# Up- and down-sampling of 1024 images on TensorE: the down-sampling goes from 128x64 to 64x64 array tiles

## The chip, the cores and the metric

One core of a Trainium2 chip runs the kernel. Its time is device time in microseconds, the median of several runs. The core has TensorE (matmuls, results in the PSUM banks), VectorE, ScalarE and GpSimd (POOL) for element work, and SyncE (SP), which here only issues DMAs. VectorE and ScalarE read PSUM; GpSimd doesn't.

## What is computed

Input x is (2, 512, 256, 256), float32. Two layers follow each other. The first adds a plane of sines to every channel:

```python
lin = jnp.einsum('oc,chw->ohw', W, coord) + b[:, None, None]   # coord: x and y in -1..1
fourier = jnp.sin(lin)
return x + fourier[None]
```

The second adds a bias per channel, up-samples by 2 with a 12-tap filter along both axes, applies a leaky ReLU (slope 0.2, times sqrt(2)), and down-samples by 2 with another 12-tap filter along both axes:

```python
out = input + bias[None, :, None, None]
out = _sep_upfirdn(out, upf, UP, 1, UP_PAD)          # 256x256 -> 512x512
out = jax.nn.leaky_relu(out, NEG_SLOPE) * FLRELU_SCALE
out = _sep_upfirdn(out, down_filter, 1, DOWN, DOWN_PAD)   # 512x512 -> 256x256
```

## The kernel before, in words

**The unit of work is an image**, one of the two batch entries of a channel; m = 2c + n is its number, c the channel and n the batch entry, 1024 in all. Each filter pass is a matmul with a band matrix: the data is the stationary operand (so that a pass also transposes), the band of filter taps (`up_band`, `down_band`, made once by VectorE, lines 369 to 381) is the moving one, and only the columns that a block of rows can reach are streamed.

**The stages of an image.** GpSimd adds x_raw and the plane f_sb into x_sum (line 245). `up_rows` (line 463) up-samples it into the two banks a_ps; ScalarE copies them to a_sb (`copy_a`). `up_cols` (line 472) up-samples a_sb into the four banks y_ps, two (a pair) at a time. ScalarE makes leak = slope x y and VectorE takes z = max(gain x y, leak) (line 392). `down_rows` (line 483) down-samples z into the bank p_ps, twice per image (i = 0, 1), and VectorE copies each half to p_rows (`copy_p`, line 400). `down_cols` (line 491) down-samples p_rows into the bank o_ps, ScalarE copies it to o_out (`copy_o`), and SP stores it.

**Array tiles.** `up` (line 439) puts 64 rows by 128 columns on the array: two tiles, one for each half of the rows. It runs in two steps (step 0 and 1), so that the two row halves never write the same bank at once; step 1 waits for a semaphore that step 0 has raised (`a_half`, `y_half`). `down` (line 428) puts 128 rows by 64 columns: two tiles, one for each half of the columns, which write different partitions of the same bank; it needs no steps. `DN_SPAN` gives the output columns that 128 input rows reach (68 or 72), `UP_SPAN` those of 128 rows going up; `up` halves the latter to 132 to 138 columns for 64 rows. All of this is float32, and the profile shows each such matmul as two loads and two matmuls.

**The plane f** is a product: sin(a+b) = sin a cos b + cos a sin b, with the bias added. `tables` (line 339) computes the sines and cosines on VectorE and ScalarE for 128 channels at a time, splits each in a high and a low float32r part (lines 360, 361), and SP saves ten rows per channel to `trig_dram` (`save_rows`). Per channel SP loads the ten rows (`load_f_rows`), `sines` (line 454) makes f in two float32r matmuls into the bank o_ps, which it shares with `down_cols`, and ScalarE copies it to f_sb (`copy_f`).

**The order.** There is no scheduler: every engine has a list written out by hand (`slot` in each engine's block), and semaphores with counted values tie them together. TensorE's slot of image m is: `up_cols` pair 0 step 0; `up_rows` of image m+1 step 0; `up_cols` pair 0 step 1; `up_cols` pair 1 step 0; `up_rows` m+1 step 1; `up_cols` pair 1 step 1; for n = 0 `sines` of channel c+1; `down_rows` of image m-1, i = 0; `down_cols` of image m-2; `down_rows` of m-1, i = 1. VectorE's slot: `leaky` 0, 1 of m, `copy_p` 0 of m-1, `leaky` 2, 3 of m, `copy_p` 1 of m-1. ScalarE's: `copy_o` of m-3, `leaky` 0, 1, `copy_a` of m+1, `copy_f` of c+1, `leaky` 2, 3. TensorE's loop (line 533) has a body of two channels, four images, and runs 254 times. `up_cols` waits for z_done, so that VectorE has read the y_ps banks of the image before. The instructions of a matmul on different tiles can pass each other on TensorE; on the other engines all goes in the order of the list.

## Time and profile before

| | us |
|---|---|
| median of 3 runs | 6572.86 (6572.68 to 6572.97) |
| the profiled execution | 6572.63 |
| its span, first to last instruction | 6570.9 |
| TensorE matmuls busy | 6509.3 (99%) |
| VectorE busy | 4002.7 (61%) |
| ScalarE busy | 3980.8 (61%) |
| GpSimd busy | 1303.7 (20%) |
| HBM traffic | 558 MB, 85 GB/s |

A row of the groups names the line, the engine, the operation, the tile written and those read, the shapes and the count; then busy us and the mean ns of one, and the idle time of the engine just before, with what ended it. PE is TensorE's matmul, PEld its weight load. Matmuls are pipelined and their ends are modelled: their starts are measured, so lengths of blocks are read here from start to start. TensorE's granted clock was full (2.4 GHz) in all slices.

### The profile page before, as it was taken

The numbers are of one execution on the slowest core, as the hardware profiler recorded it, in microseconds if no ns is written. First come the engines' busy times: TensorE is split into PE (matmuls) and PEld (weight loads), VectorE is DVE, ScalarE is ACT, GpSimd is POOL, SyncE is SP. The second block draws the span as 40 slices with busy tenths as digits, with TensorE's granted clock in tenths as the row PEclk, the third lists the DMA queues.
The fourth block names the chain that finished last, engine by engine and source line by source line (L and its number), as shares of the span: only waits on it lengthen the run. The fifth ranks groups of instructions, "written<-read, shape, count | busy, mean of one in ns | idle before, by whom it ended". The sixth has DMA issues, their size and how long they took to land.

```text
span 6570.9 us, 361569 instructions
## 1 busy us (share of the span) xinstructions
PE 6509.3 (99%) x148480; PEld 6210.1 (95%) x148480; DVE 4002.7 (61%) x6218; ACT 3980.8 (61%) x7688; POOL 1303.7 (20%) x1041
## 2 busy tenths in 40 slices
PE   6999999999999999999999999999999999999999
PEld 6999999999999999999999999999999999999999
DVE  6666666666666666666666666666666666666665
ACT  4666666666666666666666666666666666666665
POOL 2111111111111111111111111111111111111111
PEclk9999999999999999999999999999999999999999
DMA  3222222222222222222222222222222222222222
GB/s 121 85 84 84 85 85 85 84 84 83 83 84 85 85 85 85 85 85 83 85 85 85 85 83 83 83 84 85 85 85 85 85 85 83 84 85 85 85 84 78
DMA packets 580065, 558.27 MB, mean 85 GB/s; under 512 B 40400, under 2 KB 574928, under 8 KB 580048
## 3 DMA queue, kind: packets, MB, share of 16 engines
q1 hardware_dynamic: 580048, 558.02, 27.2%
q8 instruction: 14, 0.23, 0.0%
q14 instruction: 3, 0.02, 0.0%
HBM read 278.94 MB, written 278.92 MB: 85 GB/s over the span
## 4 chain that ended last, share of the span: by engine, by line
PE 99%; DVE 1%; DMA 0%; SPq 0%; issue 0%; ACT 0%; DVEq 0%; POOL 0%; POOLq 0%
PE p_ps L433 34%; PE y_ps L449 32%; PE o_ps L433 15%; PE a_ps L449 14%; PE o_ps L459 3%; DVE up_band L377 0%; DVE angle L354 0%; DVE angle L352 0%; DVE phase L344 0%; ACT trig L258 0%; DVE trig_parts L361 0%; DVE angle L356 0%; DVE turns L348 0%; DVE turns L350 0%; DVE trig_parts L360 0%
## 5 line engine op out<-in xcount | busy, mean ns | idle before, releaser
L392 DVE SCALAR_TENSOR_TENSOR z<-y_ps,leak 128x512 f32<-128x512 f32 x4096 | 2629.3, 684 | 1749.8 <-ACT leak L278 1749.8
L278 ACT ACTIVATE leak<-y_ps 128x512 f32<-128x512 f32 x4096 | 2280.0, 623 | 2108.0 <-PE y_ps L449 2107.6
L449 PE MATMUL y_ps<-up_band,a_sb 64*128 64x138 f32 (+2 forms) x32768 | 2539.2, 282 | 1.4 <-ACT a_sb L271 1.3
L433 PE MATMUL p_ps<-down_band,z 128*64 128x68 f32 (+1 forms) x65536 | 2440.8, 227 | 1.7 <-DVE p_rows L400 1.7
L245 POOL TENSOR_TENSOR x_sum<-x_raw,f_sb 128x512 f32<-128x512 f32 x1024 | 1291.3, 1283 | 5235.6 <-ACT f_sb L264 5226.3
L433 PEld LDWEIGHTS p_ps<-down_band,z 128*64 128x64 f32 x65536 | 2156.2, 137 | 160.6 <-DVE z L392 1.0
L449 PEld LDWEIGHTS y_ps<-up_band,a_sb 64*128 64x128 f32 x32768 | 2163.4, 186 | 75.1 <-issue 1.5
L400 DVE COPY p_rows<-p_ps 128x512 f32<-128x512 f32 x2048 | 1416.2, 691 | 802.3 <-PE p_ps L433 699.1
L449 PE MATMUL a_ps<-up_band,x_sum 64*128 64x138 f32 (+2 forms) x16384 | 1306.6, 275 | 28.6 <-POOL x_sum L245 28.5
L433 PE MATMUL o_ps<-down_band,p_rows 128*64 128x68 f32 (+1 forms) x32768 | 1170.2, 224 | 0.8 <-DVE p_rows L400 0.8
L449 PEld LDWEIGHTS a_ps<-up_band,x_sum 64*128 64x128 f32 x16384 | 1132.9, 187 | 29.4 <-POOL x_sum L245 29.0
L271 ACT COPY a_sb<-a_ps 128x512 f32<-128x512 f32 x2048 | 1109.4, 606 | 5.2 <-PE a_ps L449 5.2
L433 PEld LDWEIGHTS o_ps<-down_band,p_rows 128*64 128x64 f32 x32768 | 1082.4, 137 | 0.9 <-DVE p_rows L400 0.9
L283 ACT COPY o_out<-o_ps 128x512 f32<-128x512 f32 x1024 | 600.6, 587 | 432.5 <-PE o_ps L433 432.5
L264 ACT COPY f_sb<-o_ps 128x512 f32<-128x512 f32 x512 | 323.4, 632 | 0.3 <-PE o_ps L459 0.3
L459 PE MATMUL o_ps<-f_rows 10*128 10x256 f32 x1024 | 254.0, 326 | 25.8 <-DVE up_band L381 25.4
L459 PEld LDWEIGHTS o_ps<-f_rows 10*128 10x128 f32 x1024 | 149.9, 183 | 91.3 <-DVE up_band L381 25.4
L258 ACT ACTIVATE trig<-angle 128x1024 f32<-128x1024 f32 x4 | 4.2, 1056 | 40.5 <-DVE angle L356 40.5
L233 POOL TENSOR_SCALAR bias_wide<-ones,bias_high 128x256 fp32r<-128x256 f32 x4 | 5.7, 1436 | 3.7 <-DVE bias_low L334 3.7
L361 DVE TENSOR_TENSOR trig_parts<-trig,trig_parts 128x1024 f32 (+1 forms) x4 | 5.8, 1448 | 0.5
L360 DVE CAST trig_parts<-trig 128x1024 f32 (+1 forms) x4 | 2.8, 703 | 4.8 <-ACT trig L258 4.8
L377 DVE SCALAR_TENSOR_TENSOR up_band<-up_ones,up_taps,up_band 128x268 f32<-128x268 f32 x11 | 5.5, 498 | 0.4
(28 smaller groups left out, 43.0 us busy)
## 6 DMA issues: line engine op xcount, KB each, us to landing
x_raw<-in_x_dram SPq DMA_DIRECT2D x1024, 256.0 KB, 3.1
out_dram<-o_out SPq DMA_DIRECT2D x1024, 256.0 KB, 2.5
f_rows<-trig_dram SPq DMA_DIRECT2D x512, 20.0 KB
trig_dram<-trig_parts SPq DMA_DIRECT2D x32, 256.0 KB, 2.5
trig_dram<-ones SPq DMA_DIRECT2D x4, 256.0 KB, 2.4
trig_dram<-bias_wide SPq DMA_DIRECT2D x4, 256.0 KB, 2.5
up_taps<-in_L_conv_up_filter_dram SPq DMA_DIRECT2D x1, 6.0 KB, 2.3
down_taps<-_L_conv_down_filter_dram SPq DMA_DIRECT2D x1, 6.0 KB, 2.4
```

Of the source, the lines that this page charges most:

```text
L233: nc.gpsimd.tensor_scalar(bias_wide[:, t, 0, :], ones[:, 0, :], bias_high[:, t:t + 1].bitcast(f32), None, ALU.mult)
L245: nc.gpsimd.tensor_tensor(x_sum[n][:, :, :], x_raw[n][:, :, :], f_sb[:, :, :], ALU.add).then_inc(x_summed, 1)
L264: nc.scalar.copy(f_sb[:, :, :], o_ps[:, :, :]).then_inc(f_copied, 1)
L271: last = nc.scalar.copy(a_sb[n][:, t, :], a_ps[t][:, :])
L278: nc.scalar.mul(leak[i % 2][:, :], y_ps[i][:, :], SLOPE * GAIN).then_inc(leak_done, 1)
L283: nc.scalar.copy(o_out[n][:, :, :], o_ps[:, :, :]).then_inc(o_copied, 1)
L361: nc.vector.tensor_tensor(parts[:, 1, :, :], trig[:, :, :], parts[:, 0, :, :].bitcast(f32), ALU.subtract).then_inc(rows_ready, 1)
L392: nc.vector.scalar_tensor_tensor(z[n][:, i, :], y_ps[i][:, :], GAIN, leak[i % 2][:, :], ALU.mult, ALU.max).then_inc(z_done, 1)
L400: nc.vector.tensor_copy(p_rows[n][:, 2 * i:2 * i + 2, :], p_ps[:, :, :]).then_inc(p_copied, 1)
L433: last = nc.tensor.matmul(out_ps[half * HALF:(half + 1) * HALF, lo:hi], data[:, t, col:col + HALF], down_band[:, band:band + hi - lo], sta ...
L449: last = nc.tensor.matmul(outs[o][:, lo:hi], data[row, k, (at + o) * P:(at + o + 1) * P], up_band[row, band:band + hi - lo], start=step == ...
L459: last = nc.tensor.matmul(o_ps[:, t, :], f_rows[:, t * P:(t + 1) * P], f_rows[:, H:H + WID], start=True, stop=True)
```

## The change

Constants, banks and rows:

- Down-sampling is cut to 64 input rows: `DN_SPAN` has, for each of the four 128-row tiles, two spans of 36 or 40 output columns. `step_of` replaces `up` and `down`: it puts 64 rows by `cols` columns on the array, 128 columns for up-sampling, 64 (`DOWN_COLS`) for down-sampling, and runs in two steps as `up` did. Every step begins with `pe.sem_inc(steps_begun, 1)`. Up-sampling's spans are the same as before.
- p_ps gets two banks, p_ps[0] and p_ps[1], both filled only when both steps of `down_rows` have run; ScalarE copies the first (`copy_p0`), VectorE the second (`copy_p1`). The bank o_ps is gone: `down_cols` writes the left half of the two banks a_ps, and waits that ScalarE and VectorE have copied a out of them.
- a is copied by ScalarE (`copy_a0`) and VectorE (`copy_a1`), one bank each.
- The split in high and low parts is gone: f has three plain float32 rows (sine, cosine and one for the bias) instead of ten. They are loaded twice, to partitions 0 and 64 of f_rows, the rest of which GpSimd sets to zero once. `sines` runs on four 64x64 tiles into the left halves of y_ps[0] and y_ps[1], waits for z_done of the running image's first two banks, and VectorE copies it (`copy_f`). SP saves 4 times per group of channels, not 10, and loads the f rows behind the x loads and stores of a channel.

```diff
-    DN_SPAN = [(0, 68, 4), (60, 132, 0), (124, 196, 0), (188, 256, 0)]
+    DN_SPAN = [[(max(0, 32 * g - 4), min(H, 32 * g + 36), max(0, 32 * g - 4) + 4 - 64 * (g // 2)) for g in (2 * k, 2 * k + 1)]
+               for k in range(UT)]
...
-        p_ps = pb("p_ps", [P, 2, H])
-        o_ps = pb("o_ps", [P, HT, WID])
+        p_ps = [pb(f"p_ps{o}", [P, 2, H]) for o in range(2)]
```

TensorE, the common step, sines and the down-sampling:

```diff
+            def step_of(cols, outs, data, band, spans, at, where, ks, step, fresh=True):
+
+                pe.sem_inc(steps_begun, 1)
+                for k in ks:
                     for rows in range(2):
                         o = rows ^ step
                         row = slice(rows * HALF, (rows + 1) * HALF)
...
+                        lo, hi, start = spans[k][rows]
+                        for part in range(0, P, cols):
+                            col = (at + o) * P + part
+                            last = nc.tensor.matmul(outs[o][part:part + cols, lo:hi], data[row, where[k], col:col + cols],
+                                                    band[row, start:start + hi - lo],
+                                                    start=fresh and step == 0 and k == 0,
+                                                    stop=step == 1 and k == len(spans) - 1, skip_group_check=True)
                 return last
 
...
+            def sines(c, z_from):
+
+                pe.wait_ge(f_rows_loaded, 32 * c + 32)
+                reached(pe, z_done, z_from)
+                pe.sem_inc(steps_begun, 1)
                 for t in range(HT):
...
+                    row = slice(t * HALF, (t + 1) * HALF)
+                    for part in range(0, P, DOWN_COLS):
+                        col = t * P + part
+                        last = nc.tensor.matmul(y_ps[t][part:part + DOWN_COLS, 0:WID],
+                                                f_rows[row, col:col + DOWN_COLS], f_rows[row, H:H + WID],
+                                                start=True, stop=True, skip_group_check=True)
                 last.then_inc(f_made, 1)
...
+            def up_cols(m, n, pair, step, f_done=None, a_from=None):
+
                 outs = y_ps[2 * pair:2 * pair + 2]
                 if step == 0:
...
+                    if f_done is not None:
+                        pe.wait_ge(f_copied, f_done)
+                    else:
+                        reached(pe, z_done, 4 * m - 2 + 2 * pair)
...
+            def down_cols(m, n, step, a_done=None):
+                outs = [a_ps[t][:, 0:WID] for t in range(HT)]
+                if step == 0:
+
+                    if a_done is not None:
+                        pe.wait_ge(a0_copied, a_done)
+                        pe.wait_ge(a1_copied, a_done)
```

TensorE's new slot:

```diff
                 m = 2 * c + n
                 if y:
...
+                    up_cols(m, n, 0, 0, c + 2 if n == 0 and f_before else None, m + 1 if first else None)
                     up_cols(m, n, 1, 0)
                 if a_next:
+                    up_rows(m + 1, 1 - n, 0, first)
+                if y:
+                    up_cols(m, n, 0, 1)
+                if a_next:
                     up_rows(m + 1, 1 - n, 1)
                 if y:
                     up_cols(m, n, 1, 1)
-                if f_next and n == 0:
-                    sines(c + 1)
                 if p:
-                    down_rows(m - 1, 1 - n, 0)
+                    down_rows(m - 1, 1 - n, 0, 0)
+                    down_rows(m - 1, 1 - n, 0, 1)
                 if o:
-                    down_cols(m - 2, n, c + 2 if f_done is None else f_done)
+                    down_cols(m - 2, n, 0, m + 2 if a_next else None)
                 if p:
-                    down_rows(m - 1, 1 - n, 1)
+                    down_rows(m - 1, 1 - n, 1, 0)
+                if o:
+                    down_cols(m - 2, n, 1)
+                if f_next and n == 1:
+                    sines(c + 2, 4 * m + 2)
+                if p:
+                    down_rows(m - 1, 1 - n, 1, 1)
```

VectorE's new slot, with the copy of f:

```diff
+            def copy_f(c):
+
+                dve.wait_ge(f_made, c + 1)
+                reached(dve, x_summed, 2 * c)
+                for t in range(HT):
+                    last = nc.vector.tensor_copy(f_sb[:, t, :], y_ps[t][:, 0:WID])
+                last.then_inc(f_copied, 1)
+
+            def slot(c, n, a_next=True, f_next=True, y=True, p=True):
                 m = 2 * c + n
+                if a_next:
+                    copy_a1(m + 1, 1 - n)
                 if y:
                     leaky(m, n, 0)
                     leaky(m, n, 1)
-                if p:
-                    copy_p(m - 1, 1 - n, 0)
+                if f_next and n == 1:
+                    copy_f(c + 2)
                 if y:
                     leaky(m, n, 2)
                     leaky(m, n, 3)
                 if p:
-                    copy_p(m - 1, 1 - n, 1)
-
+                    copy_p1(m - 1, 1 - n)
+
```

ScalarE's new slot is `leaky` 0, `copy_a0` of m+1, `leaky` 1, 2, 3, `copy_o` of m-2 (two instructions of 256 columns), `copy_p0` of m-1. TensorE's loop body stays two channels.

## Rows read from the trace of the kernel before

**Rows 1.** The page: busy shares, the chain, and p_ps's group.

```profile
PE 6509.3 (99%) x148480; PEld 6210.1 (95%) x148480; DVE 4002.7 (61%) x6218; ACT 3980.8 (61%) x7688; POOL 1303.7 (20%) x1041
...
PE 99%; DVE 1%; DMA 0%; SPq 0%; issue 0%; ACT 0%; DVEq 0%; POOL 0%; POOLq 0%
...
L433 PE MATMUL p_ps<-down_band,z 128*64 128x68 f32 (+1 forms) x65536 | 2440.8, 227 | 1.7 <-DVE p_rows L400 1.7
```

**Rows 2.** TensorE's waits: engine, line, waited for: us, times, longest.

```profile
PE a_ps L449 <- POOL x_sum L245: 28.5, 2, 26.6
PE o_ps L459 <- DVE up_band L381: 25.4, 1, 25.4
PE p_ps L433 <- DVE p_rows L400: 1.7, 2, 0.9
```

**Rows 3.** Windows of two images: us, busy us (count) by engine, clock.

```profile
3000.03:3006.13 6.10, 6.10 (x148) 5.90 (x145) 3.88 (x7) 3.63 (x7) 0.40 (x1) 1.00 0.44 129
3006.13:3012.74 6.61, 6.61 (x151) 6.23 (x147) 3.87 (x7) 4.12 (x8) 2.13 (x2) 1.00 0.12 43
```

**Rows 4.** Timeline of one image: start us, us, instruction, count.

```profile
3000.04 0.73 PE L449 MATMUL y_ps<-up_band,a_sb 64*128 64x132 f32 x8
...
3001.06 1.10 PE L449 MATMUL y_ps<-up_band,a_sb 64*128 64x132 f32 x16
...
3001.98 0.64 PE L449 MATMUL a_ps<-up_band,x_sum 64*128 64x132 f32 x8
...
3002.55 1.29 DVE L392 SCALAR_TENSOR_TENSOR z<-y_ps,leak 128x512 f32<-128x512 f32 x2 [1.70 <-ACT leak L278]
...
3003.02 1.19 PE L433 MATMUL p_ps<-down_band,z 128*64 128x68 f32 x32
...
3004.04 1.14 PE L433 MATMUL o_ps<-down_band,p_rows 128*64 128x68 f32 x32
3004.26 0.69 DVE L400 COPY p_rows<-p_ps 128x512 f32<-128x512 f32 x1 [0.42 <-PE p_ps L433]
...
3005.02 1.18 PE L433 MATMUL p_ps<-down_band,z 128*64 128x68 f32 x32
...
3006.13 0.54 PEld L449 LDWEIGHTS y_ps<-up_band,a_sb 64*128 64x128 f32 x8
```

**Rows 5.** Timeline windows that end behind the first 2, 4, 6 loads.

```profile
3003.01 0.14 PEld L433 LDWEIGHTS p_ps<-down_band,z 128*64 128x64 f32 x2
3003.01 0.20 PEld L433 LDWEIGHTS p_ps<-down_band,z 128*64 128x64 f32 x4
3003.01 0.26 PEld L433 LDWEIGHTS p_ps<-down_band,z 128*64 128x64 f32 x6
...
3003.02 0.28 PE L433 MATMUL p_ps<-down_band,z 128*64 128x68 f32 x2
...
3006.13 0.19 PEld L449 LDWEIGHTS y_ps<-up_band,a_sb 64*128 64x128 f32 x2
3006.13 0.30 PEld L449 LDWEIGHTS y_ps<-up_band,a_sb 64*128 64x128 f32 x4
```

**Rows 6.** Timeline of the setup: the split of the sines on VectorE.

```profile
32.59 0.69 DVE L360 CAST trig_parts<-trig 128x1024 f32 x1 [1.24 <-ACT trig L258]
33.43 1.22 DVE L361 TENSOR_TENSOR trig_parts<-trig,trig_parts 128x1024 f32 x1
```

**Rows 7.** The page's groups of VectorE and ScalarE: busy us, mean ns.

```profile
L392 DVE SCALAR_TENSOR_TENSOR z<-y_ps,leak 128x512 f32<-128x512 f32 x4096 | 2629.3, 684 | 1749.8 <-ACT leak L278 1749.8
L278 ACT ACTIVATE leak<-y_ps 128x512 f32<-128x512 f32 x4096 | 2280.0, 623 | 2108.0 <-PE y_ps L449 2107.6
L400 DVE COPY p_rows<-p_ps 128x512 f32<-128x512 f32 x2048 | 1416.2, 691 | 802.3 <-PE p_ps L433 699.1
L271 ACT COPY a_sb<-a_ps 128x512 f32<-128x512 f32 x2048 | 1109.4, 606 | 5.2 <-PE a_ps L449 5.2
```

**Rows 8.** Queues, and DMA issues with the median us to landing.

```profile
q8 instruction: 14, 0.23, 0.0%
...
x_raw<-in_x_dram SPq DMA_DIRECT2D x1024, 256.0 KB, 3.1
out_dram<-o_out SPq DMA_DIRECT2D x1024, 256.0 KB, 2.5
```

## What the change is expected to do, written before it ran

> **What bounds the kernel now.** I read the busy shares and the chain first: TensorE is busy 99% of the span and carries 99% of the chain that ended last, nearly all of it on lines 449 (up-sampling) and 433 (down-sampling) [rows 1]. The waits confirm it: what TensorE waited for sums to under 60 us, and 54 of them fall once, before the first sums [rows 2]. So in steady state only two things can move the time: how long TensorE's own stretches last, and a wait that is new to it. Next the windows: an image (one batch entry of one channel) takes 6.10 us, one with the sine matmuls 6.61 [rows 3], a channel 12.71, 512 channels 6507 of the 6570.9 us span. VectorE and ScalarE are busy only 3.9 and 3.6 to 4.1 us of each image [rows 3], which looks like slack but says nothing of when they are done.
>
> The timeline of one image gives the order: the up-sampling blocks (48 records, 0.46 for every 8) go from 3000.04 to about 3002.9; three down-sampling blocks of 32 records start at 3003.02, 3004.04 and 3005.02; the next image starts at 3006.13 [rows 4]. An f32 matmul is two records (two loads, two matmuls): 65536 records of p_ps are 1024 images with 32 matmuls [rows 1]. The down part is thus 3.11 us: 48 rounds of about 0.061 (two records at once, one on each half of the columns; the round of the first stretch is (3004.04 - 3003.02 - 0.055)/16 = 0.060) and 0.15 for draining the array and the first load.
>
> **The price that decides: a weight load.** What a 64x64 round costs is not in the trace, but its two ingredients are. Columns: 138 columns on 64x128 tiles go through in a round of 0.115 (16 records in 0.92, two at once [rows 4]), 0.83 ns a column, so a 40-column record streams in 0.033. Loads: at the head of the down block two 64-column loads end 0.14 after their start, four 0.20, six 0.26 [rows 5]: each half of the array takes its next load 0.055 to 0.06 after the last one. The first of these steps cannot come from streaming, since nothing streamed yet. For 128 columns the same step is 0.11 (two end at 0.19, four at 0.30) [rows 5], so a load costs by its columns, 0.86 ns each. Before, 70 columns (0.058) just cover the 64-column load. In the changed kernel 40 columns (0.033) don't, and the load has become the longer of the two.
>
> **The change, part by part.**
> 1. Down-sampling. An image's 48 matmuls of 68 or 72 columns become 96 of 36 or 40, 192 records. Four at a time that is 48 rounds, as many as before: only the round's length changes. If loads of four tiles run side by side (the trace shows it for two column halves and for two row halves, not for four), a round is 0.055 to 0.060; I take 0.057. 48 x 0.057 = 2.74 + 0.15 = 2.89 against 3.11: 0.22 saved per image, 0.44 per channel. The bounds from rows are 0.033 (streaming alone) and 0.110 (only two loads at a time).
> 2. Sines. Two records of 256 columns and a mode of their own cost 6.61 - 6.10 = 0.51 per channel [rows 3]. Now four f32 matmuls of 256 columns on four tiles, two passes of 256 x 0.83 = 0.21, 0.43 together, in the mode of their neighbours: 0.08 saved.
> 3. Up-sampling keeps its spans, tiles and number: 0. Its order changes (both first halves go ahead); each second half still has a block between itself and what it waits for, 0.46 or more, against some 0.2 from last column to a reader's start (p_ps block ends at 3004.04, VectorE's copy starts 4.26 [rows 4]): hidden. The new p and o half steps have a 0.46 block between them too. If that cover were gone, each would cost up to 0.2.
> 4. Copies. VectorE loses one p copy and gets half of a (one 0.69 each), and f in two of 256 columns; per channel 12 x 0.605 + 0.68 = 7.9 of 12.7 (0.605 is the step from one 512-column instruction to the next: two end 1.29 after the first starts, one takes 0.69 [rows 4, 7]). ScalarE has 4 leaks, one a, one p and two o halves: 4 x 0.62 + 2 x 0.61 + 2 x 0.35 = 4.4 of 6.1 at most [rows 7]. POOL does the same sums. Throughput of each is covered. o now waits for a_sb to be out of a_ps: a_ps is full 2.4 us into the image, both copies are done at 3.3 (0.2 and 0.69 later), and the o step starts at 2.9 + 0.2 + 2 x 0.456 = 4.0: hidden, with 0.7 to spare.
> 5. Semaphore steps: 12 or 13 more sequencer instructions per image, and 290 records per image become about 480. Now a block's 32 loads and 32 matmuls are fed in 0.97 [rows 4]; then it must be in 0.456. In 0.02 us two loads and two matmuls start [rows 5], so the engine accepts them in bursts; I take 0, bound 0.1 per image (+100 us in all), and a gain is excluded.
> 6. Setup: the split of the sines in two parts goes, 0.7 + 1.2 to 1.3 us for each of four groups on VectorE [rows 6], which stand before the first sum: -8 us. SP: 4 saves for 10, f rows in two DMAs for one, now issued behind the next x loads and stores; the rows are needed 12 us later and a landing takes some 3 [rows 8]: 0.
>
> Sum without waits: 12.71 - 0.44 - 0.08 = 12.19 per channel, -266 us.
>
> **7. The wait that the change adds.** f now goes through y_ps[0..1], is made by `sines` late in the second image of each channel (behind the o half steps, ahead of the last p block), and is copied by VectorE. In VectorE's order `copy_f` stands between `leaky` 1 and `leaky` 2 of that same image. VectorE is through with `leaky` 1 some 4.5 us into the image and then waits for f until about 6.0, with the `leaky` 2, 3 and the p copy of this image queued behind it, although their y is ready. TensorE needs them at once: `up_cols` step 0 of pair 0 in the next image waits for f_copied, that of pair 1 for all four z. Set the end of the sines to 0:
> - copy_f starts at 0.22 (the 0.22 of point 3), two copies of 256 columns 2 x 0.34 (half of the 0.605 step and some for its start), f_copied at about 1.0;
> - z2 starts at 0.90, z3 at 1.50, ends at 2.19 (0.69 [rows 7]), seen by TensorE at 2.24;
> - TensorE without waits: last p block to 0.46, drain and first load 0.20 (from 3006.13 back to the end of the columns, and 0.11 for the 128-column load), so up_cols pair 0 at 0.55 and pair 1 at 1.12.
> So pair 0 waits 0.48 and pair 1 the rest, 1.12 together, and 0.1 for a weight load laid bare behind the second wait: 1.2 per channel, +625 us. Nothing is late behind that: the rest of the image runs as the sum has it, since its z and copies have slack again.
>
> 12.19 + 1.22 = 13.41, +0.70 per channel, x 512 = +358; 6572.6 (the profiled execution's own time, beside a median of 6572.9) + 358 - 8 = 6923, and with a little of point 5, **6930 us**. A round of 0.055 gives 6830, one of 0.060 and the full point 5 give 7170.
>
> **Rivals.**
> - **Instruction memory (B), 7250.** The queue of instructions moved 14 packets, 0.23 MB, in the whole run [rows 8]: the loop's body is fetched once and kept. That body is 4 images x 290 = 1160 instructions; the new one is 4 x 480 + 32 = 1952 and some 100 for semaphores and registers. If it isn't kept, each of 254 passes waits for its first part: a DMA's way from issue to landing is 2.5 to 3.1 us [rows 8], during which the 1.1 of point 7 passes too. Net 1.0 to 1.6 a pass, +250 to +400 on 6930: 7180 to 7330. The trace shows a body of 1160 kept and no more. [...]
> - **Loads don't bind (C), 6380 to 6490: the other side.** If a 64x64 tile's load is cheaper than a half array's, a round is 0.036 to 0.045. The down part is then 1.7 to 2.2 and the sum without waits 10.2 to 11.0, but z of the upper half then arrives late in every image: the chain from the last y block over ScalarE's leaks and VectorE's z to the next image's pair 1 costs 0.5 in each image beside point 7. With the same durations, step by step as in point 7, a channel takes 12.33 to 12.54. It decides from a round under 0.046. Against it: loads cost by their columns in rows 5, and the tile's columns stay 64. The Trainium skill, "TensorEngine Tiling (Array Packing)", Tiling Modes, says that different tiles can load and multiply in parallel, its Theoretical Speedup gives up to 2x for each dimension that is 64 or less, and its PSUM Bottleneck names the copies as what may bind next. By that rule alone this case would hold.
> - **The wait of point 7 is hidden (E), 6520 to 6580.** If VectorE got z2 and z3 done ahead of f, pair 1 wouldn't wait: 12.65 per channel. The order in the code speaks against it.
> - **Four tiles don't run at once (D), about 9300.** If only two of the loads or records go side by side, a round is 0.110: 48 x 0.05 more per image. The trace shows two at once along either side of the array, and a program order of four instructions per tile that is overtaken for one other tile; three others would have to be reached.
>
> **How the numbers follow.** The forecast (A) 0.43, B 0.23, C 0.13, E 0.06, D 0.15. A's own range is 6830 to 7170. The range that leaves out D and some of C and of the ends is 6400 to 7400. About 0.2% is what a measurement of this kernel can tell from no change; E straddles that. Faster 0.17 (C and most of E), same 0.02, slower 0.81.
>
> **What would show it.** In the timeline of the changed kernel: blocks of 32 records at 0.44 to 0.48 apart in the down part (right: A; 0.3: C; 0.9: D); VectorE idle before copy_f for some 1.5 us each channel, released by the sines; waits of y_ps on VectorE's f_sb (about 0.5 x 512) and z (about 0.6 x 512) in TensorE's list; windows near 6.1 and 7.3 for the two images of a channel. The instruction queue's packets stay near 20 (A) or go to thousands (B), with a gap at the start of every fourth image. I am wrong if the loads of a tile don't cost by columns, or if the last two z are not behind f.

## The result and the profile after

The changed kernel takes **11206.6 us** (11195.7 to 11216.6, 4 runs) against 6572.9 before (6572.7 to 6574.1): the ratio is **1.705, 95% interval 1.702 to 1.708**. The forecast was 6930 with a range of 6400 to 7400; the sign was right, the size wrong by more than 4000 us. Of the 4634 us lost, 4066 come from something that the forecast's sum put at nothing, as the first experiment shows; the other 568 are the loss that it describes.

The page of the changed kernel (busy shares, clock, the instruction queue, the chain):

```profile
PE 8078.5 (72%) x249856; PEld 7506.8 (67%) x249856; DVE 4281.8 (38%) x7232; ACT 4104.5 (37%) x8200; POOL 1308.7 (12%) x1038
...
PEclk9888888888888888888888888888888888888888
...
q8 instruction: 2300, 37.68, 1.3%
...
PE 69%; issue 27%; DVE 4%; DVEq 1%; ACT 0%; DMA 0%; SPq 0%; POOL 0%; ACTq 0%; POOLq 0%
```

TensorE, 99% busy before [rows 1], is busy 72%. The chain now has 27% "issue": time in which TensorE waited for nothing that the profile shows. And the instruction queue, which moved 14 packets before [rows 8], moves 2300. TensorE's waits (engine, line, waited for: us in total, times, longest), which summed to under 60 us before [rows 2]:

```profile
PE y_ps L451 <- issue: 870.4, 253, 3.9
PE y_ps L466 <- issue: 765.3, 509, 2.1
PE a_ps L451 <- issue: 637.4, 512, 1.8
PE p_ps L451 <- issue: 629.4, 491, 1.9
PE y_ps L451 <- DVE f_sb L402: 114.0, 258, 1.1
PE y_ps L451 <- DVE z L388: 61.8, 132, 1.7
```

The four "issue" rows sum to 2902.5 us, 11.4 for each of the 254 passes of the loop; what the forecast was about, the waits for f and z, is 176 us. A stretch of TensorE's timeline shows where the gaps are (start us, us, instruction, count; in brackets the idle time ahead). It begins with the branch at the loop's end:

```profile
6025.40 1.02 PE L451 MATMUL p_ps<-down_band,z 64*64 64x40 f32 x24
6029.62 2.19 PE L451 MATMUL y_ps<-up_band,a_sb 64*128 64x132 f32 x16 [3.19 <-issue]
6031.55 1.16 PE L451 MATMUL a_ps<-up_band,x_sum 64*128 64x132 f32 x8
6032.45 1.17 PE L451 MATMUL y_ps<-up_band,a_sb 64*128 64x132 f32 x8
...
6037.33 0.63 PE L451 MATMUL a_ps<-down_band,p_rows 64*64 64x36 f32 x26
6039.21 0.32 PE L451 MATMUL a_ps<-down_band,p_rows 64*64 64x40 f32 x6 [1.24 <-issue]
...
6045.05 0.60 PE L451 MATMUL p_ps<-down_band,z 64*64 64x36 f32 x27 [1.36 <-issue]
```

Three things are to be seen. First, the gap at 6029.62 stands at the branch; those at 6039.21 and 6045.05 break off in the middle of a block of equal matmuls (32 of a_ps are cut in 26 and 6), where no wait stands in the code. My reading is that TensorE has run out of instructions; the experiments test it. Second, apart from the branch, the down-sampling part with the sines in it is where this happens. Third, the up-sampling blocks behind the long gap follow each other at 0.90 us and not at the 0.46 of before [rows 4]: the granted clock, 1.00 in all of before, is 0.867 here, and a pass from branch to branch has 0.81:

```profile
6025.73:6070.76 45.03, 33.17 (x994) 30.78 (x988) 16.59 (x28) 16.03 (x32) 5.08 (x4) 0.81 0.17 50
...
6025.73:6035.36 9.63, 6.43 (x70) 6.08 (x64) 3.23 (x7) 1.89 (x4) 1.95 (x2) 0.50 0.10 32
```

(us; busy us and count of PE, PEld, DVE, ACT, POOL; clock; DMA share and GB/s.) The low clock, 0.50, comes in two stretches of this pass: up to 6035.36, where it is already down at the branch, behind a stop in the sines (1.65 us, up to 6024.89), and again from 6048.95 to 6055.83 (0.52, TensorE busy for 6.64 us), behind a stop of 1.83 in the sines. The shorter stops at 6039.21 and 6045.05 leave it at 1.00. In the two stretches TensorE is busy for 13.1 us; at an up block's 0.46 for 0.90 about half of that, some 6.4 us, is the price of the clock (an estimate from these rows). This pass of two channels took 45.0 us; before, it was 25.4. Its instruction packets start at 6026.74, 6030.28, 6036.68, 6042.62, 6046.30, 6050.14, 6057.85, 6063.48 and 6067.18: nine, of 16.4 KB each (37.68 MB by 2300), for a body of some 2,040 instructions, taking 0.93 to 1.28 us each. TensorE goes on 2.2 to 2.9 us after the start of a packet it was waiting for (6057.85 to 6060.05: 2.20; 6036.68 to 6039.21: 2.53; 6026.74 to 6029.62: 2.88).

### The profile page after: what moved, and what is told of

The parts are those of the page before. It is cut to its first block, busy times and chain, and to the rows that moved or that the text cites. A ratio compares the mean times of both kernels' runs of the same rounds, so it can differ in the third digit from the quotient of the medians.

```text
span 11214.8 us, 576531 instructions
## 1 busy us (share of the span) xinstructions
PE 8078.5 (72%) x249856; PEld 7506.8 (67%) x249856; DVE 4281.8 (38%) x7232; ACT 4104.5 (37%) x8200; POOL 1308.7 (12%) x1038
## 3 DMA queue, kind: packets, MB, share of 16 engines
q8 instruction: 2300, 37.68, 1.3%
## 4 chain that ended last, share of the span: by engine, by line
PE 69%; issue 27%; DVE 4%; DVEq 1%; ACT 0%; DMA 0%; SPq 0%; POOL 0%; ACTq 0%; POOLq 0%
PE y_ps L451 25%; PE a_ps L451 22%; PE p_ps L451 18%; PE y_ps L466 4%; DVE f_sb L402 2%; DVE z L388 1%; DVEq L137 0%; DVEq L385 0%; DVEq L425 0%; DVE up_band L367 0%; DVE angle L346 0%; DVE angle L348 0%; DVE phase L338 0%; ACT trig L258 0%; DVE turns L342 0%
## 5 line engine op out<-in xcount | busy, mean ns | idle before, releaser
L451 PE MATMUL y_ps<-up_band,a_sb 64*128 64x138 f32 (+2 forms) x32768 | 3377.5, 341 | 1046.3 <-issue 870.4
L451 PEld LDWEIGHTS y_ps<-up_band,a_sb 64*128 64x128 f32 x32768 | 2944.7, 240 | 1165.0 <-issue 1142.3
L451 PE MATMUL p_ps<-down_band,z 64*64 64x40 f32 (+1 forms) x131072 | 2811.3, 228 | 631.1 <-issue 629.4
L451 PEld LDWEIGHTS p_ps<-down_band,z 64*64 64x64 f32 x131072 | 2490.8, 137 | 885.5 <-issue 733.5
L451 PE MATMUL a_ps<-down_band,p_rows 64*64 64x40 f32 (+1 forms) x65536 | 1553.2, 226 | 638.4 <-issue 637.4
L381 DVE COPY a_sb<-a_ps 128x512 f32<-128x512 f32 x1024 | 707.7, 691 | 3358.2 <-PE a_ps L451 3358.2
L451 PEld LDWEIGHTS a_ps<-down_band,p_rows 64*64 64x64 f32 x65536 | 1313.5, 135 | 698.9 <-issue 698.9
L277 ACT COPY o_out<-a_ps 128x256 f32<-128x256 f32 x2048 | 662.0, 375 | 1915.0 <-PE a_ps L451 1915.0
L466 PE MATMUL y_ps<-f_rows 64*64 64x256 f32 x4096 | 540.4, 449 | 789.4 <-issue 765.3
L284 ACT COPY p_rows<-p_ps 128x512 f32<-128x512 f32 x1024 | 609.9, 596 | 1220.6 <-PE p_ps L451 1220.4
L395 DVE COPY p_rows<-p_ps 128x512 f32<-128x512 f32 x1024 | 701.2, 685 | 918.9 <-PE p_ps L451 918.9
```

Source lines behind the costliest of these rows:

```text
L277: last = nc.scalar.copy(o_out[n][:, t, :], a_ps[t][:, 0:WID])
L284: nc.scalar.copy(p_rows[n][:, 0:2, :], p_ps[0][:, :, :]).then_inc(p0_copied, 1)
L381: nc.vector.tensor_copy(a_sb[n][:, 1, :], a_ps[1][:, :]).then_inc(a1_copied, 1)
L395: nc.vector.tensor_copy(p_rows[n][:, 2:4, :], p_ps[1][:, :, :]).then_inc(p1_copied, 1)
L451: last = nc.tensor.matmul(outs[o][part:part + cols, lo:hi], data[row, where[k], col:col + cols], band[row, start:start + hi - lo], start=f ...
L466: last = nc.tensor.matmul(y_ps[t][part:part + DOWN_COLS, 0:WID], f_rows[row, col:col + DOWN_COLS], f_rows[row, H:H + WID], start=True, sto ...
```

## The experiments

A body's size is given in TensorE's instructions, counted in the traces from branch to branch with the semaphore and register instructions. The kernel before has 1,208 (1,210 below), the changed kernel 2,036 (2,040). The expectations were written with somewhat higher figures: 1,030 for 1,019, 2,050 for 2,036, 2,430 for 2,414 and 1,880 for 1,811.

**One channel in the loop's body.** The changed kernel with a body of some 1,020.

```diff
-    PE_CHANNELS = 2
+    PE_CHANNELS = 1
```

> The changed kernel with TensorE's loop body cut from two channels to one (PE_CHANNELS = 1; every instruction and wait is the same, the body is some 1,030 instructions in place of some 2,050). Theory 1 (instruction memory: the body of two channels is fetched again in each pass, 2300 packets, and TensorE runs dry because a block of 64x64 instructions is used up faster than the next one comes): the queue of instructions falls from 2300 packets to some 20, the gaps put down to issue go, the clock is back at 1.0, and the time is that of the sum without rival B, 6930 (6830 to 7170). Theory 2 (64x64 tiles themselves are slow, or the added waits are, and the fetches are beside the point): stays above 9000. Inside theory 1: the rounds of four loads are 0.055 to 0.060 us, and TensorE waits some 1.1 us per channel for VectorE's f_sb and z.

Measured: 7140.9 us (7139.5 to 7143.4), 1.087 times before (1.085 to 1.088), clock 0.998. The instruction queue, TensorE's waits and the part of the timeline around the second sum of a channel:

```profile
q8 instruction: 19, 0.31, 0.0%
...
PE y_ps L451 <- DVE f_sb L402: 314.1, 511, 1.1
PE y_ps L451 <- DVE z L388: 235.9, 511, 1.4
```

```profile
3001.74 0.73 PE L451 MATMUL y_ps<-up_band,a_sb 64*128 64x132 f32 x8 [0.61 <-DVE f_sb L402]
3002.93 0.73 PE L451 MATMUL y_ps<-up_band,a_sb 64*128 64x132 f32 x8 [0.46 <-DVE z L388]
3003.47 0.66 PE L451 MATMUL a_ps<-up_band,x_sum 64*128 64x132 f32 x8
...
3005.45 1.14 PE L451 MATMUL p_ps<-down_band,z 64*64 64x36 f32 x64
...
3007.80 0.65 PE L451 MATMUL p_ps<-down_band,z 64*64 64x36 f32 x32
3008.38 1.20 PE L451 MATMUL y_ps<-up_band,a_sb 64*128 64x132 f32 x16
...
3013.25 0.65 PE L451 MATMUL a_ps<-down_band,p_rows 64*64 64x36 f32 x32
3013.78 0.66 PE L466 MATMUL y_ps<-f_rows 64*64 64x256 f32 x8
3014.23 0.65 PE L451 MATMUL p_ps<-down_band,z 64*64 64x36 f32 x32
3015.49 0.73 PE L451 MATMUL y_ps<-up_band,a_sb 64*128 64x132 f32 x8 [0.61 <-DVE f_sb L402]
```

With the shorter body nothing is fetched again, the gaps are gone and so is the low clock: one number in the code is worth 4066 us. What is left, +568, is the case that the forecast describes (13.76 per channel on the average, 3001.74 to 3015.49 here; its own range was 6830 to 7170). The 4066 split by the two pages: gaps 2903, TensorE's busy time 8078.5 - 6516.9 = 1562 more for the same instructions (the lower clock: 6.1 a pass, where the estimate above is 6.4), and 374 less waiting for f and z (176 for 550): 4091 in sum, 25 off.

**The copy of f last.** On top of that, VectorE's copy of f behind `leaky` 3.

```diff
-                if f_next and n == 1:
-                    copy_f(c + 2)
                 if y:
                     leaky(m, n, 2)
                     leaky(m, n, 3)
+                if f_next and n == 1:
+                    copy_f(c + 2)
```

> As e1, and VectorE copies f behind leaky 2 and 3 of its image, not ahead of them (one line of its slot moved). Point 7 of the prediction: the second of the two waits (for z, some 0.64 and a load of 0.1 per channel) goes, the first (for f_sb, 0.48) stays: 12.65 to 12.7 us per channel, 380 us under e1, about 6550. Rival: the waits cost nothing or lie elsewhere: same time as e1.

Measured: 6766.0 us (6763.5 to 6767.7), 1.030 (1.028 to 1.031); 13.03 per channel. The step, 375 us, is the 380 expected; the level is 215 above the number, because the run it started from was. The wait for z is gone (2.3 us in all), that for f stays at 313.8: TensorE asks for f first.

**Pair 1 first.** On top of that, `up_cols` step 0 of pair 1 ahead of that of pair 0 in the first image of a channel (and y_half waits to suit), so that f has one more block of time.

```diff
-                    pe.wait_ge(y_half, 2 * m + pair + 1)
+                    pe.wait_ge(y_half, 2 * m + (2 if n == 0 else pair + 1))
...
+                    if n == 0 and not first:
+                        up_cols(m, n, 1, 0)
+                        up_cols(m, n, 0, 0, c + 2 if f_before else None)
...
```

> As e2, and in the first image of a channel TensorE begins with pair 1 of up_cols and does pair 0, which waits for f, second (the waits for y_half are raised to match). If the rest of point 7 holds, the wait for f_sb (0.48 per channel) is covered by the 0.46 block of pair 1: 12.2 us per channel, about 6310, which would be 4% under the kernel before. Rival: something else of the down part (sequencer instructions, a longer round) holds it: 6450 to 6600.

Measured: 6543.4 us (6541.5 to 6545.0), 0.9955 (0.9938 to 0.9971): under before, but by 29 us, not 260; in the size a miss. The waits on f and z are gone (1.7 and 2.3 us in all) and another has come, at the branch:

```profile
PE y_ps L451 <- issue: 87.0, 506, 0.2
```

```profile
3004.73 0.65 PE L451 MATMUL p_ps<-down_band,z 64*64 64x36 f32 x32
3005.55 1.20 PE L451 MATMUL y_ps<-up_band,a_sb 64*128 64x132 f32 x16 [0.17 <-issue]
...
3010.88 0.65 PE L451 MATMUL p_ps<-down_band,z 64*64 64x36 f32 x32
3011.47 1.20 PE L451 MATMUL y_ps<-up_band,a_sb 64*128 64x132 f32 x16
```

From the last down block's start to the first up block's it is 0.82 across the branch and 0.59 in the middle of the body: 0.23 per channel, 120 us. Nothing is fetched there (19 packets in the whole run). My reading is that the branch with its register work takes longer than the short matmuls already in the queue last; in the kernel before, whose matmuls last twice as long, the first block behind a branch (3018.83) starts as soon after its predecessor as any other, 0.15.

**The branch in the up-sampling part.** The loop is cut behind the first three up blocks, where a block has 16 instructions for the sequencer in 0.46 us and not 64.

```diff
+                if part == 1:
+                    return
...
+            slot(2, 0, part=1)
             with pe.Fori(2, C - 2, PE_CHANNELS) as c:
-                for k in range(PE_CHANNELS):
-                    slot(c + k, 0)
-                    slot(c + k, 1)
-            slot(C - 2, 0)
+                slot(c, 0, part=2)
+                slot(c, 1)
+                slot(c + 1, 0, part=1)
+            slot(C - 2, 0, part=2)
```

> As e3_pair1_first, with TensorE's loop cut at another place: the body begins behind the first three up-sampling blocks of an image, so that the branch falls between 64x128 blocks and not behind the last 64x64 block. The same instructions in the same order. In e3 the first block of every channel starts 0.39 after the last 64x64 record and not 0.15, behind a branch and register work of 0.47 us on TensorE's sequencer, whose queue lasts only 0.23 us at the 64x64 rate. At the 64x128 rate a full queue lasts 0.46. Theory: the 0.23 per channel goes, 6543 - 512 x 0.23 = 6425. Rival: the queue isn't full there either and the same 0.2 shows up inside the up part: 6540.

Measured: 6580.2 us (6569.2 to 6582.8, 11 runs), 1.001 (1.0001 to 1.0019); 12.64 per channel on the average in the trace. A miss: it is 37 us over the run before, where 118 less had been expected. The 0.23 behind the last down block is gone, and the next item took its place:

```profile
3002.23 0.65 PE L451 MATMUL p_ps<-down_band,z 64*64 64x36 f32 x32
3002.81 1.42 PE L451 MATMUL y_ps<-up_band,a_sb 64*128 64x132 f32 x16
3004.03 0.66 PE L451 MATMUL a_ps<-up_band,x_sum 64*128 64x132 f32 x8
```

The first up block starts 0.58 after the last down block, but its 16 records (pairs 1 and 0) and what follows them need 1.22 where 1.00 is normal (3005.55 to 3006.55 above). Between its two halves stands the wait for the copy of f: VectorE ends the copy at 3003.35, TensorE's sequencer gets past the wait at 3003.39, and the first load of the second half is 0.1 later. f is now the last to arrive; in the run before, the branch had given it 0.23 of time. The two runs are thus even here (0.58 + 1.22 = 1.80 for 0.82 + 1.00 = 1.82). The branch, now at 3003.97, is not quite free either: a block behind it takes 0.50 (3004.49 to 3004.99) for 0.46. The rest of the 37 us is open.

**f third.** On top of that, the first up blocks of the image in the order pair 1, `up_rows`, pair 0: one more block for f.

```diff
+                        up_cols(m, n, 1, 0)
+                        up_rows(m + 1, 1 - n, 0, first)
+                        up_cols(m, n, 0, 0, c + 2 if f_before else None)
...
```

> As e6_branch_in_up_part, and in the first image of a channel the up-sampling blocks go pair 1 step 0, up_rows step 0, pair 0 step 0 (the one that waits for f), up_rows step 1, pair 0 step 1, pair 1 step 1; the loop is cut behind the third. e6 was no faster than e3: its second block still starts 0.22 after the one ahead and not 0.07 to 0.1, because f_copied comes only then, so the time gained at the branch was given back to the wait for f. Theory: with one more block of 0.46 ahead of it the wait is covered, and the 0.2 per channel at the branch stays gained: 12.58 - 0.2 = 12.38 per channel, 6440. Rival: y of pair 0 comes one block later now, leaks and z are late for the next image, and TensorE waits for z: 6540 or more.

Measured: **6514.9 us** (6511.5 to 6519.4), **0.9913 (0.9899 to 0.9926)**: the best of all, 58 us under before (under 1%); expected were 6440, or 6540 and more if z came late. Its timeline, with VectorE's z behind it:

```profile
3003.66 0.73 PE L451 MATMUL y_ps<-up_band,a_sb 64*128 64x132 f32 x8
...
3009.58 1.37 PE L451 MATMUL y_ps<-up_band,a_sb 64*128 64x132 f32 x16
3010.75 0.66 PE L451 MATMUL a_ps<-up_band,x_sum 64*128 64x132 f32 x8
...
3016.19 0.73 PE L451 MATMUL y_ps<-up_band,a_sb 64*128 64x132 f32 x8
...
3007.97 2.10 DVE L388 SCALAR_TENSOR_TENSOR z<-y_ps,leak 128x512 f32<-128x512 f32 x3 [0.20 <-ACT leak L271]
```

The first image is at its floor (5.92, with nothing waited for). In the second, the first 16 records need 1.17 and not 1.03: pair 1 waits for its z, the last of which VectorE ends at 3010.07, as the third in a row behind ScalarE's leaks; TensorE's sequencer gets past that wait at 3010.11. A channel takes 12.53 against 12.33 for two images of 5.91 and the sines' 0.51.

**Four channels in the body, kernel before.** Some 2,410 instructions, and none of the change.

```diff
-    PE_CHANNELS = 2
-    assert (C - 2) % PE_CHANNELS == 0
+    PE_CHANNELS = 4
+    assert (C - 4) % PE_CHANNELS == 0
```

> The kernel before with TensorE's loop body of four channels in place of two (some 2,430 instructions, nothing else changed). Theory 1 says that a body over what is kept is fetched again in each of 127 passes, some 10 packets each, 1200 to 1300 in all; its 128x64 and 64x128 instructions take 15 ns or more each, so a block of 256 lasts 4 us, longer than a fetch, and only the branch back stalls: about 3 us, and some 1.5 more at the lower clock behind it, per pass: 6573 + 127 x 3 to 4.5 = 6950 to 7150. Rival (a fetch costs at every block, also here): 10 gaps of 1.5 us per pass, 8400. Rival (size isn't it): 6573, some 20 packets.

Measured: 7254.3 us (one run), clock 0.958.

```profile
q8 instruction: 1404, 23.00, 1.4%
...
PE y_ps L449 <- issue: 409.2, 126, 3.6
```

The packets come back without any 64x64 tile, eleven a pass, but there is one gap a pass, 3.2 us, at the branch. TensorE's busy time is 6782.2, 273 above before; 409 + 273 = 682 is the whole loss (7254.3 - 6572.8 = 681.5). That is 5.4 us a pass, and 104 us over the top of what was expected: the gaps alone would have given 6982, inside it, and the rest is the clock.

**Three channels in the body, kernel before.** Some 1,810 instructions, 169 passes (one more channel ahead of the loop to make the count fit).

```diff
-    PE_CHANNELS = 2
+    PE_CHANNELS = 3
...
+            slot(3, 0)
+            slot(3, 1)
+            with pe.Fori(4, C - 1, PE_CHANNELS) as c:
```

> The kernel before with TensorE's loop body of three channels (some 1,880 instructions; one more channel stands ahead of the loop, which runs 169 times). It brackets the size from which a body is fetched again: 1,210 instructions are kept (the kernel before), about 2,050 (the changed kernel) and 2,430 (e4) are not. If what counts is 2048 instructions in all, 1,880 may be kept: 6573 and some 20 packets. If a body that touches nine blocks of 256 with the one asked for ahead is too much, it is fetched again: some 9 x 169 = 1500 packets, and one stop of 3.2 us and 2.1 us of lower clock per pass as in e4 (5.4 a pass): 6573 + 169 x 5.4 = 7480.

Measured: 7500.0 us (one run), clock 0.943.

```profile
q8 instruction: 1530, 25.07, 1.5%
...
PE y_ps L449 <- issue: 552.3, 168, 3.7
```

Nine packets a pass: 1,810 isn't kept either, and the time is near the 7480 expected for that case. 552 of gaps and 375 of busy time (6884.7 against 6509.3) are the 927 lost, 5.5 a pass as with four channels.

**Down-sampling on 64x128 tiles, two channels in the body.** The half steps and the order of the change, but half as many, wider loads, and so a body of some 1,250.

```diff
-    DOWN_COLS = 64
+    DOWN_COLS = 128
```

> The changed kernel with DOWN_COLS = 128: down-sampling and sines on 64x128 tiles, half as many instructions, each with the same 36 or 40 columns but a load of 128 columns. Its two-channel body is some 1,250 instructions and should be kept (some 20 packets). This is the disputed price by itself. If a load costs by its columns and binds (0.11 for 128), a round of two is 0.110 to 0.115 and a 16-record block of the down part takes 0.88 to 0.92: 17.3 to 18.0 us per channel, 9000 to 9300. If streaming bound it (40 columns, 0.033 to 0.040), such a block would take 0.3 and the kernel 6400 to 6700.

Measured: 10558.5 us (one run), clock 0.834. The instruction queue moves 14 packets in all, and TensorE is hardly ever idle (its wait for f is 0.22 a channel, 113.9 in all):

```profile
PE 10382.0 (98%) x149504; PEld 10232.9 (97%) x149504; DVE 4285.1 (41%) x7232; ACT 4107.1 (39%) x8200; POOL 1306.2 (12%) x1038
```

```profile
3005.18 1.09 PE L451 MATMUL a_ps<-down_band,p_rows 64*128 64x36 f32 x16
...
3008.75 2.05 PE L451 MATMUL y_ps<-up_band,a_sb 64*128 64x132 f32 x16
3010.52 1.19 PE L451 MATMUL a_ps<-up_band,x_sum 64*128 64x132 f32 x8
...
3012.32 0.69 PE L451 MATMUL a_ps<-up_band,x_sum 64*128 64x132 f32 x8
```

A down block of 16 records takes 0.893 (four from 3005.18 to 3008.75), a round of 0.112 with 36 or 40 columns to stream: it is the 128-column load, as [rows 5] priced it (0.11). Six of them are 5.4 for 2.8 on 64x64, which gives the 9000 to 9300 that was expected. The time itself is a miss, and the rest are the up blocks: two from 3010.52 to 3012.32, 0.90 each, and only then 0.46. An up part, from 3008.75 to the next down block at 3013.27, takes 4.52 for 2.98, 1.54 more in each of 1024 images, 1577 us. The windows show the clock doing it (columns as above):

```profile
3003.48:3008.75 5.27, 5.27 (x100) 5.27 (x97) 3.05 (x5) 2.73 (x6) 1.15 (x1) 1.00 0.00 0
3008.75:3012.32 3.57, 3.57 (x36) 3.57 (x36) 0.69 (x1) 0.65 (x2) 0.00 (x0) 0.53 0.47 147
```

So the clock falls to its half level (1.2 of 2.4 GHz) without any idle time, behind a stretch in which loads set the pace and little was streamed, and comes back in the course of the up part (0.98 from 3012.32 to 3013.27). DMA traffic is high in the slow window too (0.47), but in the kernel before a window with 0.44 had the full clock [rows 3].

**Wide down matmuls, two channels in the body, then one.** To tell whether a block's gap is a fixed price or only what consumption leaves uncovered, the down matmuls are given 144 columns of `up_band`, so that the same 2,040 instructions take longer. Their results are not the down-sampled image then; only the time is read.

```diff
+                        if cols == DOWN_COLS:
+                            lo, hi, start, band = min(lo, H - 144), min(lo, H - 144) + 144, 0, up_band
```

The second run has this and `PE_CHANNELS = 1`.

> The changed kernel (body of two channels, fetched again in every pass) with every 64x64 down-sampling matmul streaming 144 columns of up_band in place of 36 or 40 of down_band: the same number of instructions, loads, waits and fetches, more columns; p and o are not what the reference asks for. A round of four becomes 0.12 (144 columns at 0.83 ns), so 256 instructions last 3.8 us in place of 1.9. Theory 1a (the next 16 KB come one block ahead and arrive 3.3 to 3.9 us after they are asked for; only blocks that run out sooner leave gaps): the gaps in the down part go, that at the branch stays; 4 x 2.96 us more streaming and some 11 us less gap and cold clock per pass: about the time of the changed kernel, 11000 to 11700. Theory 1b (every block costs a fixed stop of some 1.5 us): all gaps stay, 45 + 12 = 57 us per pass, 14400.

> As e8 (144 columns in each 64x64 down-sampling matmul, so p and o are not what the reference asks for) with the body of one channel, which is kept. The base for e8: e1 and 2 x 2.96 per channel, less some waits that are covered now: 19 to 19.7 us per channel, 9800 to 10200. e8 minus this run is what the fetches cost when the instructions are slow: theory 1a some 5 us per pass of two channels (one stop at the branch and the clock behind it), 1300 us in all; theory 1b 4200.

Measured: 11409.1 us with two channels (clock 0.924) and 9982.8 with one (clock 1.000), one run each, both as expected (11000 to 11700, 9800 to 10200). With two:

```profile
q8 instruction: 2553, 41.83, 1.7%
...
PE y_ps L453 <- issue: 977.4, 253, 4.5
```

Ten packets a pass, one more than in the changed kernel, but all gaps except the one at the branch are gone (the next row by "issue" is 0.3 us in all). The difference is 1426 us, 5.6 a pass (1300 had been expected, 4200 if every fetch cost its stop), of which 977 are gaps and 587 busy time (10228.0 against 9640.9), less 117 of waits (1447 in sum, 21 off). Within the body a fetch costs TensorE nothing here: 256 instructions of the down part last 3.9 us now (a block of 64 takes 0.98) and lasted 1.9 before.

## Why the prediction was wrong

**The step that failed is the fetching of instructions: the forecast's sum put it at nothing, and rival B, which names it, had too low a price and too low a chance.** B has 1.0 to 1.6 us a pass, net; measured are 16.0 (4066 us by 254), 11.4 of them gaps and 6.1 the clock, less waits. B's mechanism was named, and its sign in the profile ("packets go to thousands, with a gap at the start of every fourth image") came true. Two things in it were wrong.

*The size.* It was priced as one stop of 2.5 to 3.1 us per pass, with the rest fetched unseen behind it. (Less the 1.1 of point 7 that is 1.4 to 2.0, not the 1.0 to 1.6 written there; the slip is small beside the rest.) For a body that TensorE uses slowly that is nearly right: the kernel before with four or three channels in its body stops once a pass, 3.2 to 3.3 us. But the working never asked how long 256 instructions last, which is what the section cited below gives as the block that is fetched (the packets here have 16.4 KB). In the up part, 8 matmuls and 8 loads take 0.46, so a packet lasts over 7 us; in the down part 32 and 32 take 0.467, so it lasts 1.9 us, less than the 2.2 to 2.9 from a packet's start to TensorE's going on. Hence 11.4 us of gaps per pass: 3.4 at the branch (870.4 by 253) and 8.0 in the down parts. In the down part the change halves the columns per instruction and doubles the number of instructions; both make this worse, and both numbers stood in point 5 (32 loads and 32 matmuls fed in 0.97 before and in 0.456 after). The Trainium skill, "Runtime: NRT & Kernel Launch", Instruction fetch mechanics, says that instructions come in blocks of 256 and that crossing from one block to the next is "mostly hidden". By the rows above that holds for the wide matmuls and for the kernel before with a long body, and not for narrow matmuls on four tiles (8.0 us a pass).

*The chance.* B was given 0.23. The same section of the Trainium skill gives TensorE room for 2048 instructions; the changed kernel's 2,036 are fetched again, and 1,811 as well, so here that figure isn't the limit for a loop's body. Kept were 1,020, 1,210 and 1,250. The prediction itself noted that the trace showed 1,160 kept and no more (1,210, with the semaphore and register instructions); for a body 1.7 times that, it had no ground to call keeping the likelier case.

**The lower clock** stood in no case: 1562 us of the 4066. It goes with the gaps: the same instructions without them have 0.998 (with one channel in the body). Even the kernel before, with one gap of 3.2 us a pass, loses another 2.1 to 2.2 us a pass in busy time (273 by 127, 375 by 169).

The other steps can be judged in the run with one channel in the body, where the forecast's own case is realised:

- **Point 1, down-sampling:** the round is 0.467 by 8 = 0.0583, predicted 0.057. The load sets the pace, four tiles do run at once (rivals C and D are out), and a down part is 2.93 us (3005.45 to 3008.38) for 3.11; 2.89 had been predicted. The gain is 0.18 per image for 192 matmul records, and as many loads, in place of 96.
- **Point 2, sines:** 0.08 was to be saved; nothing is. From the o block's start to the sines' is 0.53 and on to the last p block 0.45, 0.98 where the one block alone would take 0.467: 0.51, what it was before [rows 3].
- **Point 3, up-sampling:** from the first up block to the first down block 2.98 (3008.38 to 3011.36), as before [rows 4]. Right.
- **Point 5, sequencer:** 0 per image was nearly right inside the body, and wrong at the branch: 0.23 per channel once the waits on f no longer cover it.
- **Point 6, setup:** 8 us less was expected; the first matmul of the first sum starts at 52.92, and at 52.81 before. The split that went was not what the first sum waited for. 0 saved.
- **Point 7, the wait for f:** 1.2 per channel was predicted, in two parts, for f and z. TensorE's list has 1.07 (550 by 512). By starts, the first block comes 0.68 late (1.26 behind the start of the last down block, for 0.58), the second 0.63 (1.19 for 0.56), 1.31 in all, and the block behind the waits another 0.08. The mechanism was right in each step: VectorE is idle in front of the copy of f and z 2, 3 follow it, in the one-channel run:

```profile
3014.59 0.76 DVE L402 COPY f_sb<-y_ps 128x256 f32<-128x256 f32 x2 [1.61 <-PE y_ps L466]
3015.27 1.28 DVE L388 SCALAR_TENSOR_TENSOR z<-y_ps,leak 128x512 f32<-128x512 f32 x2
```

Together: 12.71 - 2 x 0.19 + 1.31 + 0.08 = 13.72 of the measured 13.76, where the prediction had 13.41. The 0.3 too little is point 7 by 0.2 and point 2 by 0.08; the rest is the rounds.

The remedy of each wait showed the next one: z behind f (375 us), f itself (223, where some 120 more were then lost at the branch), then the branch and f together (29 by the last version). What the change can bring with all of them gone is 512 x 0.38 = 195 us, or 3%; the best kernel has 58 of that.

**What stays open:** where between 1,250 and 1,810 instructions the body stops being kept, and whether the count or the place of the body in the program decides; no run lies between them. Why the stop at the branch is 3.9 us with wide matmuls and 3.2 to 3.4 otherwise. Exactly when the clock falls: the runs show it behind single gaps of 3.2 us, behind some of the 1.65 to 1.83 and behind a stretch bound by loads without any, not what these have in common. And the 0.2 us per channel by which the best kernel misses its floor, of which 0.14 stand between the first two blocks of the second image, read from the timeline and not tested.

## What to carry to other kernels

Before a loop's body is made longer, or its matmuls smaller, count TensorE's instructions in it and how long 256 of them last. If the body outgrows what is kept (here a limit between 1,250 and 1,810) and a stretch of it uses 256 faster than the next come, TensorE starves there; here it did at 1.9 us for 256, and not at 3.9. The body should be shortened first then; the sign is the instruction queue's packets on the page and idle time by "issue". Smaller array tiles gain only down to the load of a tile: with 36 to 40 float32 columns on 64x64 the 64-column load of 0.058 us sets the pace, and the number of instructions in the down part has doubled.

## What the runs showed of the hardware

- A body was either kept or fetched anew in full on every pass: 14 to 19 packets in all at 1,020 to 1,250 instructions, 9 or 10 per pass at 1,810 and 2,040, 11 at 2,410.
- The stop at a branch to a place that isn't kept is 3.2 to 3.4 us on the average (409.2 by 126; 552.3 by 168; 870.4 by 253), and 3.9 with the wide matmuls (977.4 by 253).
- Within a body that isn't kept, TensorE stops for 1.2 to 1.5 us on the average where it uses 256 instructions in 1.9 us (765.3 by 509, 637.4 by 512, 629.4 by 491), and not at all where they last 3.9 us.
- The granted clock fell to 0.53 in a stretch behind one in which TensorE and its loads were busy without a gap at 1.00, with 36 to 40 columns streamed per 128-column load; a busy TensorE is no safeguard of its clock.
- A taken branch of a kept body costs 0.23 us behind a 64x64 block (64 instructions in 0.47 us), and nothing in the kernel before, where 64 last twice as long.
